# Combining the experts inside the second cross attention's program

## Chip, cores and metric

The kernel runs on one core of one Trainium2 chip. The metric is the device time of one execution in microseconds (us); lower is better. The engines are TensorE (PE in the profile; PEld is its weight load), VectorE (DVE), ScalarE (ACT), GpSimd (POOL) and SyncE (SP), which issues most of the DMAs. Each engine runs its own list of instructions in order; semaphores tie the lists together. SBUF is the memory on the chip, PSUM the banks into which TensorE writes.

## What is computed

A decoder of two layers over x, 4 x 1024 tokens of 256 numbers. Each half layer adds to x a function of its layer norm:

```python
x = x + _L0_xattn_ref(_layernorm(x), ctx, ctx, mask, ...)
x = x + _L0_ffn_ref(_layernorm(x), ...)      # self-attention, then one of 8 experts per token
x = x + _L1_xattn_ref(_layernorm(x), ctx, ctx, ...)
x = x + _L1_ffn_ref(_layernorm(x), ...)
```

What bears on the change is the end of the second and the start of the third:

```python
# end of _L0_ffn_ref: src is the attention's output, sel the chosen expert's row of each token
moe = sel * jnp.sum(wts, axis=-1, keepdims=True)
return _ln(src + moe, n2_g, n2_b)
# _L1_xattn_ref
query = _split_heads(q @ Wq + bq)            # q = _layernorm(x); 16 heads of 16
key_ = _split_heads(k @ Wk + bk)             # k = v = ctx, 64 rows per batch
value = _split_heads(v @ Wv + bv)
logits = jnp.einsum('bhqd,bhkd->bhqk', query, key_) / jnp.sqrt(DEPTH)
attn = jax.nn.softmax(logits, axis=-1)
out = jnp.einsum('bhqk,bhkd->bhqd', attn, value)
return concat @ Wo + bo
```

## The kernel before

x stays in SBUF as 32 tiles of 128 tokens; the stages go over it in eight chunks of four tiles (512 tokens). Each stage is a program of its own (a `Block`): all engines start it together and leave it together, and the semaphores are cleared in between.

`combine_experts` (names `co_`) ends the second half layer. SyncE loads the experts' rows chunk by chunk (`yg`), with the scale `n2g` after the second chunk and, behind all chunks, the seven tensors of the next cross attention's context (`Context.issue`: weights, transposed context, biases). VectorE forms z = rows x weight + src (`co_z`) and its moments, two chunks ahead of the rest; GpSimd makes the reciprocal deviation; VectorE turns mean and deviation into a shift; ScalarE normalizes z in place; GpSimd multiplies by `n2g`; VectorE adds z to x.

`cross_attention` (names `xa_`) follows. Its front: VectorE takes the moments of x, GpSimd makes `rstd`, VectorE normalizes x into `xn` (`normalize_x`), TensorE transposes it into the PSUM tile `front` (`transpose_xn`), ScalarE evacuates that to `xnT`, TensorE projects queries into the PSUM tile `rows` in two halves (`project_q`), ScalarE evacuates each half with its bias into `qT`. TensorE begins with the keys and values, which need only the context; ScalarE places the keys into a block form (`place_keys`) between the evacuations. TensorE's order is: transpose chunk 0; then for each chunk c transpose c+1, project c. A half of the projection waits for the evacuation of the same half one chunk earlier, since `rows` has one bank for each.

After the last projection come the four row maxima of chunk 0 (`scores` on TensorE, `maximum` on VectorE, turn by turn over the one tile `rows`), and then `attend(c)` for each chunk. It begins with `transpose_max`, writes the transposed scores to `cols`, and ScalarE makes the exponentials `pT`. GpSimd adds the output bias to x for all eight chunks (`add_output_bias`) after the last `rstd`.

The same function serves the first cross attention, which has a mask and takes x from the inputs.

Of the kernel before, what the change touches and what calls it, by code (L numbers as in the profile page):

```python
# [101 lines left out]
def cross_attention(nc, x_sb, k_, context, mask, name):  # L102
# [4 lines left out]
    with ExitStack() as ctx:  # L107
# [15 lines left out]
        qT = sb("qT", [P, HALVES, TOKENS])  # L123
# [6 lines left out]
        rden = sb("rden", [P, P])  # L130
        front = ps("front", [P, HALVES, CW])
# [14 lines left out]
        q_banks = [rows[:, half] for half in range(HALVES)]  # L146

        with nc.Block() as block:
            @block.sync
            def _(sp):  # L150
                if not context.issued:
                    context.issue(sp)
                if masked:
                    sp.dma_start(mask_i[:], mask.rearrange("(t p) k -> p t k", p=P)).then_inc(mask_loaded, 16)
# [3 lines left out]
            def _(dve):  # L158
# [95 lines left out]
                moments(0)  # L254
                moments(1)
                place_key_bias()
                for c in range(CHUNKS):
                    normalize_x(c)
                    if c == 0:
                        place_values()  # L260
                    if c + 2 < CHUNKS:
                        moments(c + 2)
                    if c == 1:
                        place_fill()
                for t in range(CT):
                    maximum(0, t)
# [8 lines left out]
            def _(pool):  # L275
# [40 lines left out]

                nc.gpsimd.memset(vblk[:], 0.0).then_inc(v_cleared, 1)
                for c in range(CHUNKS):
# [14 lines left out]
            def _(act):  # L333
# [6 lines left out]
                def evacuate_qT(c, half):  # L340
                    act.wait_ge(q_psum, 2 * c + half + 1)
                    nc.scalar.activation(qT[:, half, CW * c:CW * (c + 1)], q_banks[half], ACT.Identity,
# [33 lines left out]
                evacuate_xnT(0)  # L376
                act.wait_ge(context.loaded, context.count)
                act.wait_ge(kbias_made, 1)
                for c in range(CHUNKS):
# [24 lines left out]
            def _(pe):  # L404
# [27 lines left out]
                def scores(c, t):  # L432
# [9 lines left out]
                    for half in range(HALVES):  # L442
                        for r in range(2):
                            part = slice(SC * r, SC * (r + 1))
                            last = nc.tensor.matmul(rows[:, r, half * D:(half + 1) * D], qT[part, half, tokens],  # L445
# [15 lines left out]
                def weights_of(c, half):  # L461
# [9 lines left out]
                    for g in range(4):  # L471
                        part = slice(32 * g, 32 * (g + 1))
                        nc.tensor.matmul(cols[:, g], kblk[part, c // 2, half, 2 * g:2 * g + 2], qT[part, half, tokens],
# [79 lines left out]
                transpose_xn(0)  # L553
                for c in range(CHUNKS):
                    if c + 1 < CHUNKS:
                        transpose_xn(c + 1)
                    project_q(c)
# [9 lines left out]
                for t in range(CT):  # L567
# [2161 lines left out]
```

## Time and profile before

| | us |
|---|---|
| median of 3 runs (lowest to highest) | 1999.68 (1997.29 to 2002.81) |
| the profiled execution, its own time | 2008.15 |
| span of its trace | 2006.4 |
| combine_experts, from the engines' start on it to its last addition | 1397.8 to 1451.0 |
| change of program | 1451.0 to 1453.0 |
| front of the second cross attention | 1453.0 to 1507.0 |
| four maxima of its first chunk | 1507.0 to 1518.0 |
| its eight chunks of attention | 1518.0 to about 1668 |

Of these stretches the busy times are, for TensorE, 0, 0, 46.7, 5.5 and 139.6 us; for VectorE 45.6, 0, 39.6, 5.8 and 68.6 us.

A row of the views in order of time reads: start, duration, engine, line, operation, output<-inputs, shape, count of instructions merged into the row, and in brackets how long the engine had been idle before it and what ended that. Times are counted from the start of the span. Matmuls in fp32 appear as two instructions each, and their ends are modelled, so that neighbouring rows overlap a little. A row of the views by stretch gives the length, the busy time and count of each engine (PE, PEld, DVE, ACT, POOL), the granted TensorE clock as a share of full speed, the DMA share, and GB/s.

### The profile page before, as it was taken

What the parts mean: (1) busy time and instruction counts of PE and PEld (TensorE: products, weight loads), DVE (VectorE), ACT (ScalarE), POOL (GpSimd) and SP (SyncE); (2) the same over time, 40 slices, a digit from 0 to 9 for tenths busy, and PEclk for the clock granted to TensorE, in tenths of its full rate; (3) what the DMA queues carried; (4) which work ended last, traced back from release to release, by engine and by line L of the source; (5) the groups of instructions that cost most, each with busy time, mean ns of one, the idle gap of its engine ahead of it and who ended that gap; (6) DMA issues with size and microseconds to landing.
All of it is one profiled execution on the core that took longest, in us unless ns stands there. A gap on an engine that the chain in (4) does not pass through costs nothing. (4 is left out here: it accounts for less than half of the span.)

```text
span 2006.4 us, 30050 instructions
## 1 busy us (share of the span) xinstructions
PE 1703.1 (85%) x10580; PEld 805.3 (40%) x10580; DVE 1256.7 (63%) x2123; ACT 962.7 (48%) x1803; POOL 598.9 (30%) x645
## 2 busy tenths in 40 slices
PE   5899799899999999999997966996088996239996
PEld 3466454222222222222222653774054663125554
DVE  5344358788888888888860774664874545661221
ACT  2432245488888888888885422443342332102110
POOL 4300063242221121121121373665660002021533
PEclk8899999899999999999998977998588997658998
DMA  5000059532222322222102422222300004310542
GB/s 141 1 2 1 19 167 304 198 75 39 39 39 38 64 50 38 39 39 39 39 2 98 153 81 79 65 66 73 96 1 1 1 1 140 126 33 15 140 108 32
DMA packets 112677, 134.51 MB, mean 67 GB/s; under 512 B 18480, under 2 KB 88496, under 8 KB 112272
## 3 DMA queue, kind: packets, MB, share of 16 engines
q1 hardware_dynamic: 101824, 114.20, 20.8%
q0 software_dynamic: 9552, 17.83, 3.7%
q8 instruction: 87, 1.43, 0.3%
q10 hardware_dynamic: 1152, 0.54, 0.1%
q14 instruction: 62, 0.51, 0.1%
HBM read 78.47 MB, written 53.93 MB: 66 GB/s over the span
## 5 line engine op out<-in xcount | busy, mean ns | idle before, releaser
L892 DVE TENSOR_REDUCE sa_mhalf<-sa_a 128x2 f32<-128x1024 f32 x512 | 604.3, 1221 | 84.4 <-PE sa_a L1104 82.7
L1037 ACT ACTIVATE sa_e<-sa_b 128x512 f32<-128x512 f32 x683 | 383.4, 601 | 76.9 <-PE sa_b L1137 76.9
L1147 PE MATMUL sa_b2o<-sa_e,sa_v 128*17 128x512 f32 x2048 | 269.7, 598 | 0.0
L1037 ACT ACTIVATE sa_e<-sa_b2o 128x512 f32<-128x512 f32 x341 | 205.0, 601 | 40.6 <-PE sa_b2o L1137 40.6
L1137 PE MATMUL sa_b<-sa_q,sa_k 112*128 112x512 bf16 x468 | 163.4, 388 | 2.7 <-ACT sa_e L1037 2.7
L840 POOL TENSOR_TENSOR sa_rden<-sa_o_rows,sa_minus_one 128x16 f32<-128x16 f32 x32 | 93.0, 2908 | 178.1 <-ACT sa_o_rows L1020 178.1
L213 DVE TENSOR_REDUCE xa_mx<-xa_rows 128x16 f32<-128x1024 f32 x64 | 78.3, 1224 | 100.2 <-PE xa_rows L445 100.2
L1104 PE MATMUL sa_a<-sa_k,sa_q 48*128 48x512 bf16 x704 | 113.3, 389 | 13.2 <-DVE sa_mhalf L892 13.2
L829 POOL CAST sa_negm<-sa_neg 16x128 bf16<-16x128 f32 x32 | 9.4, 293 | 348.7 <-issue 338.9
L360 ACT ACTIVATE xa_pT<-xa_cols 128x1024 f32<-128x1024 f32 x64 | 62.1, 1022 | 84.5 <-PE xa_cols L477 84.5
L1137 PEld LDWEIGHTS sa_b<-sa_q,sa_k 112*128 112x128 bf16 x468 | 40.6, 97 | 151.2 <-ACT sa_e L1037 134.4
L1137 PE MATMUL sa_b2o<-sa_q,sa_k 112*128 112x512 bf16 x236 | 91.3, 387 | 0.6 <-ACT sa_e L1037 0.5
L2611 DVE TENSOR_TENSOR sw_hT<-sw_p,sw_act 128x512 f32<-128x512 f32 x32 | 22.1, 692 | 101.1 <-PE sw_p L2556 101.1
L2524 POOL DMA_INDIRECT out_x<-sw_yo,tc_idx x32 | 49.9, 1560 | 104.7 <-DVE sw_yo L2618 97.7
L1697 PE MATMUL ex_hps<-at_w,ex_xT 128*128 x156 | 77.3, 619 | 1.9 <-ACT ex_xT L1737 1.9
L445 PE MATMUL xa_rows<-xa_kblk,xa_qT 64*128 64x256 f32 x512 | 73.1, 407 | 6.1 <-DVE xa_mx L213 5.3
L1104 PEld LDWEIGHTS sa_a<-sa_k,sa_q 48*128 48x128 bf16 x704 | 30.5, 93 | 114.7 <-issue 56.7
L2600 ACT ACTIVATE sw_act<-sw_p 128x512 f32<-128x512 f32 x32 | 19.1, 597 | 118.0 <-PE sw_p L2550 115.2
L1720 PE MATMUL ex_yps<-at_attn,ex_hT 128*128 x312 | 74.0, 380 | 0.5 <-ACT ex_hT L1747 0.4
L544 PE MATMUL xa_cols<-c_ctxT,c_wts 128*128 128x256 f32 x16 | 7.5, 652 | 77.9 <-PEq L43 64.2
L1137 PE MATMUL sa_b<-sa_parts 112*128 112x512 bf16 x215 | 73.5, 384 | 0.0
L1747 ACT ACTIVATE ex_hT<-ex_tps,at_bt,at_g 128x128 f32<-128x128 f32 x156 | 58.8, 457 | 15.8 <-PE ex_tps L1708 15.8
(345 smaller groups left out, 3066.3 us busy)
## 6 DMA issues: line engine op xcount, KB each, us to landing
k_parts<-sa_parts SPq DMA_DIRECT2D x96, 128.0 KB, 2.2
tc_w<-in_L_ffn_W SPq DMA_DIRECT2D x24, 512.0 KB
sa_q<-q_parts SPq DMA_DIRECT2D x44, 192.0 KB, 5.4
sa_k<-k_parts SPq DMA_DIRECT2D x44, 192.0 KB, 5.8
q_parts<-sa_parts SPq DMA_DIRECT2D x16, 384.0 KB
ex_xg<-expert_in SPq DMA_DIRECT2D x39, 132.0 KB
v_groups<-sp_vt SPq DMA_DIRECT2D x8, 544.0 KB, 4.6
sa_v<-v_groups SPq DMA_DIRECT2D x16, 272.0 KB, 7.6
```

The source lines that it names most:

```text
L213: nc.vector.tensor_reduce(mx[:, t], rows[:].rearrange("p r (n k) -> p (r n) k", k=SC), axis=X, op=ALU.max).then_inc(max_done, 1)
L360: nc.scalar.activation(pT[:, 4 * half + 2 * part:4 * half + 2 * part + 2], cols[:, 2 * part:2 * part + 2], ACT.Exp, scale=SCALE).then_inc( ...
L445: last = nc.tensor.matmul(rows[:, r, half * D:(half + 1) * D], qT[part, half, tokens], kblk[part, c // 2, half, CT * r:CT * (r + 1)], star ...
L840: nc.gpsimd.tensor_tensor(rden[:], view[:, :, :, DK], minus_one[:], ALU.pow).then_inc(rden_made, 1)
L892: nc.vector.tensor_reduce(mhalf[a % 2][:, half, head:head + PAIRED + 1:PAIRED, t], aps[a_slot(use)][:], axis=X, op=ALU.max).then_inc(a_use ...
L1037: nc.scalar.activation(ex[(KT * n + kt) % (LAG + 1)][:, head], bps[use % 3], ACT.Exp, scale=SCALE).then_inc(b_used, 1)
L1104: last = nc.tensor.matmul(aps[a_slot(use)][:, h // PAIRED], qs[s][rows, h, q0:q0 + P], ks[s][rows, h, half * CW:(half + 1) * CW], start=Tr ...
L1137: nc.tensor.matmul(bps[use % 3], ks[s][:, head, kt * P:(kt + 1) * P], qs[s][:, head, qc * CW:(qc + 1) * CW], start=True, stop=True).then_i ...
L1147: last = nc.tensor.matmul(ops[32 * head:32 * head + VW], vs[s][:, kt, head], ex[(KT * n + kt) % (LAG + 1)][:, head], start=(kt == 0), stop ...
L1697: last = nc.tensor.matmul(hps[j % 2][:], xT[j % 2][:, half], ew["w1"][:, half, ds(e, 1), :], start=(half == 0), stop=(half == HALVES - 1))
L1720: last = nc.tensor.matmul(yps[j % 2][:, 0:D], hT[j % 2][:, f], ew["w2"][:, f, ds(e, 1), :], start=(f == 0), stop=(f == FK - 1))
L1747: last = nc.scalar.activation(hT[j % 2][:, f], tps[j % 2][:, f * P:(f + 1) * P], ACT.Gelu, bias=ew["bt"][:, f, ds(e, 1)], scale=ew["g"][:, ...
```

## The change

`combine_experts` is gone as a program. `cross_attention` gets an argument `combine`, which the second one is called with, and does the combination in its own program:

- z lies in what will be `pT`, the experts' rows in what will be `qT`, which is now ordered by chunk. The projection writes to the first two banks of `cols` in place of `rows`.
- SyncE issues the context's loads behind the third chunk of rows instead of behind the eighth.
- VectorE goes through steps: the shift of chunk s, the sum of chunk s+2, the addition to x and the moments of x for chunk s-1, a second shift (`xshift`) for chunk s-2. The key bias is made in step 2, the values placed in step 4, and from step 6 on each step ends with one maximum of chunk 0.
- ScalarE normalizes x too (`normalize_rows`, with `xshift`); before, VectorE did.
- ScalarE's step s is: normalize z of chunk s; in steps 2 and 3 place eight keys, in step 2 after waiting for the key bias; evacuate `xnT` of chunk s-3; normalize x of chunk s-2; evacuate the two query halves of chunk s-4.
- TensorE transposes chunk c, then projects chunk c; after chunks 1 to 4 the scores of one of chunk 0's four tiles follow.
- GpSimd makes the selector first, then the deviations of z and x and the multiplication, in steps; the two other constant shapes and the eight bias additions come after that.

The core of the diff:

```diff
-        qT = sb("qT", [P, HALVES, TOKENS])
+        qT = sb("qT", [P, CHUNKS, HALVES, CW])
...
-        q_banks = [rows[:, half] for half in range(HALVES)]
+        q_banks = [(cols if combine else rows)[:, half] for half in range(HALVES)]
...
+                if combine:
+                    for c in range(CHUNKS):
+                        sp.dma_start(yg[c], moe_out[CW * c:CW * (c + 1)].rearrange("(t p) d -> p t d", p=P)).then_inc(y_loaded[c], 16)
+                        if c == 1:
+                            sp.dma_start(n2g[:], n2_g.partition_broadcast(P)).then_inc(g_loaded, 16)
+                        if c == 2:
+                            context.issue(sp)
...
+                if combine:
+                    weighted_sum(0)
+                    weighted_sum(1)
+                    for step in range(CHUNKS + 2):
+                        if step < CHUNKS:
+                            make_shift(step)
+                        if step + 2 < CHUNKS:
+                            weighted_sum(step + 2)
+                        if 1 <= step <= CHUNKS:
+                            add_experts(step - 1)
+                            moments(step - 1)
+                        if step >= 2:
+                            make_x_shift(step - 2)
+                        if step == 2:
+                            place_key_bias()
+                        if step == 4:
+                            place_values()
+                        if step >= 6:
+                            maximum(0, step - 6)
...
+                    invert(0)
+                    pool.wait_ge(g_loaded, 16)
+                    for step in range(CHUNKS + 1):
+                        if step + 1 < CHUNKS:
+                            invert(step + 1)
+                        if step < CHUNKS:
+                            scale(step)
+                        if step >= 1:
+                            make_rstd(step - 1)
...
+                def normalize_rows(c):
+                    par = c % 2
+                    act.wait_ge(xshift_ready, c + 1)
+                    act.wait_ge(rstd_ready, c + 1)
+                    act.wait_ge(x_done, c + 1)
+                    if c >= 2:
+                        act.wait_ge(xnT_psum, c - 1)
+                    for t in range(CT):
+                        nc.scalar.activation(xn[:, par, t], x_sb[:, CT * c + t], ACT.Identity, bias=xshift[:, par, t:t + 1],
+                                             scale=rstd[:, par, t:t + 1]).then_inc(xn_ready, 1)
+
+                if combine:
+                    for step in range(CHUNKS + 4):
+                        if step < CHUNKS:
+                            normalize_z(step)
+                        if step == 2:
+                            act.wait_ge(kbias_made, 1)
+                        if 2 <= step < 4:
+                            act.wait_ge(k_psum, step - 1)
+                            for h in range(HH):
+                                place_keys(step - 2, h)
+                        if 3 <= step < CHUNKS + 3:
+                            evacuate_xnT(step - 3)
+                        if 2 <= step < CHUNKS + 2:
+                            normalize_rows(step - 2)
+                        if step >= 4:
+                            for half in range(HALVES):
+                                evacuate_qT(step - 4, half)
...
+                if combine:
+                    for c in range(CHUNKS):
+                        transpose_xn(c)
+                        if c == 0:
+                            pe.wait_ge(kblk_made, H)
+                        project_q(c)
+                        if 1 <= c <= CT:
+                            pe.wait_ge(qT_ready, HALVES)
+                            scores(0, c - 1)
+                else:
+                    transpose_xn(0)
+                    for c in range(CHUNKS):
+                        if c + 1 < CHUNKS:
+                            transpose_xn(c + 1)
+                        project_q(c)
```

On TensorE, from the key projection of the second cross attention, the order before is this (`xnT0` and `xnT1` are the two buffers of transposed x; the first entry of a row is the line, the last the count):

```order
L544 MATMUL xa1_cols<-c1_ctxT,c1_wts 128x256 x4
L550 MATMUL xa1_cols<-c1_wts,c1_ctxT 128x256 x8
L411 MATMUL xa1_front<-x_ident,xa1_xn 128x128 x16
L421 MATMUL xa1_rows<-xa1_xnT0,c1_wts 128x512 x4
L411 MATMUL xa1_front<-x_ident,xa1_xn 128x128 x8
L421 MATMUL xa1_rows<-xa1_xnT1,c1_wts 128x512 x4
```

Sixteen transposes, of chunks 0 and 1, stand ahead of the first projection. And now, at the same place:

```order
L693 MATMUL xa1_cols<-c1_ctxT,c1_wts 128x256 x4
L699 MATMUL xa1_cols<-c1_wts,c1_ctxT 128x256 x8
L560 MATMUL xa1_front<-x_ident,xa1_xn 128x128 x8
L570 MATMUL xa1_cols<-xa1_xnT0,c1_wts 128x512 x4
L560 MATMUL xa1_front<-x_ident,xa1_xn 128x128 x8
L570 MATMUL xa1_cols<-xa1_xnT1,c1_wts 128x512 x4
L594 MATMUL xa1_rows<-xa1_kblk,xa1_qT 128x256 x4
```

The transposes of chunk 1 have moved behind the projection of chunk 0, and scores follow the second projection.

On ScalarE, from the normalization of z, the order before is this:

```order
L1905 ACTIVATE co_z<-co_z,co_shift,co_rstd 128x256 x32
L1864 UNCONDITIONAL_BRANCH
L332 UNCONDITIONAL_BRANCH
L338 ACTIVATE xa_xnT<-xa_front 128x1024 x2
L342 ACTIVATE xa_qT<-xa_rows,c_bqk 128x512 x2
L347 ACTIVATE xa_kblk<-xa_cols,xa_kbias,x_headmask 128x4x64 x4
L338 ACTIVATE xa_xnT<-xa_front 128x1024
L342 ACTIVATE xa_qT<-xa_rows,c_bqk 128x512 x2
```

and now (z is `xa_pT`):

```order
L492 ACTIVATE xa_pT<-xa_pT,xa_shift,xa_zrstd 128x256 x12
L457 ACTIVATE xa_kblk<-xa_cols,xa_kbias,x_headmask 128x4x64 x8
L503 ACTIVATE xa_xn<-x_x,xa_xshift,xa_rstd 128x256 x4
L492 ACTIVATE xa_pT<-xa_pT,xa_shift,xa_zrstd 128x256 x4
L457 ACTIVATE xa_kblk<-xa_cols,xa_kbias,x_headmask 128x4x64 x8
L448 ACTIVATE xa_xnT<-xa_front 128x1024
L503 ACTIVATE xa_xn<-x_x,xa_xshift,xa_rstd 128x256 x4
L492 ACTIVATE xa_pT<-xa_pT,xa_shift,xa_zrstd 128x256 x4
L448 ACTIVATE xa_xnT<-xa_front 128x1024
L503 ACTIVATE xa_xn<-x_x,xa_xshift,xa_rstd 128x256 x4
L452 ACTIVATE xa_qT<-xa_cols,c_bqk 128x512 x2
```

All sixteen key placements now come ahead of the second evacuation of transposed x, and a normalization of x stands between each evacuation of transposed x and the evacuation of query halves.

On SyncE the context's loads stood behind the eighth chunk of rows:

```order
L1868 DMA co_yg<-moe_out 128x4x256 x2
L1871 DMA co_n2g<-in_L_ffn_n_g 128x256
L1868 DMA co_yg<-moe_out 128x4x256 x6
L98 DMA c_wts<-in_L_xattn_wts 128x8x256
L98 DMA c_ctxT<-in_ctxT 128x4x64 x4
```

and now they stand behind the third (the rows go into `xa_qT`):

```order
L164 DMA xa_qT<-moe_out 128x4x256
L98 DMA c_wts<-in_L_xattn_wts 128x8x256
L98 DMA c_ctxT<-in_ctxT 128x4x64 x4
L98 DMA c_bqk<-in_L_xattn_bqk 128x4
L98 DMA c_bv<-in_L_xattn_bv 128x256
L98 DMA c_bo<-in_L_xattn_bo 128x256
L164 DMA xa_qT<-moe_out 128x4x256 x5
```

The last five chunks have moved behind seven loads.

## Rows read from the trace of the kernel before

**Rows 1.** VectorE in order of time: start, us, engine, line, operation.

```profile
1401.76 1.67 DVE L1915 SCALAR_TENSOR_TENSOR co_z<-co_yg,sm_wsum,sm_src 128x256 f32<-128x256 f32 x4 [12.32 <-DMA co_yg<-moe_out]
...
1404.95 1.64 DVE L1915 SCALAR_TENSOR_TENSOR co_z<-co_yg,sm_wsum,sm_src 128x256 f32<-128x256 f32 x4
...
1415.99 2.39 DVE L1941 TENSOR_TENSOR x_x<-x_x,co_z 128x1024 f32<-128x1024 f32 x1
...
1441.85 1.23 DVE L1941 TENSOR_TENSOR x_x<-x_x,co_z 128x1024 f32<-128x1024 f32 x1
...
1453.04 1.41 DVE L188 BATCH_NORM_STATS2 xa_stats<-x_x 128x6 f32<-128x256 f32 x4 [2.06 <-PEq L43]
1454.36 0.37 DVE L194 BATCH_NORM_AGGREGATE xa_mv<-xa_stats 128x2 f32<-128x6 f32 x4
...
1481.60 14.89 DVE L203 TENSOR_SCALAR xa_xn<-x_x,xa_mv,xa_rstd 128x256 f32<-128x256 f32 x8 [0.78 <-PE xa_front L411]
```

**Rows 2.** ScalarE in order of time.

```profile
1408.26 2.07 ACT L1905 ACTIVATE co_z<-co_z,co_shift,co_rstd 128x256 f32<-128x256 f32 x4 [21.57 <-DVE co_shift L1933]
...
1467.77 1.02 ACT L338 ACTIVATE xa_xnT<-xa_front 128x1024 f32<-128x1024 f32 x1 [4.40 <-PE xa_front L411]
1470.29 0.69 ACT L342 ACTIVATE xa_qT<-xa_rows,c_bqk 128x512 f32<-128x512 f32 x1 [1.50 <-PE xa_rows L421]
...
1472.60 1.93 ACT L347 ACTIVATE xa_kblk<-xa_cols,xa_kbias,x_headmask 128x256 f32<-128x256 f32 x4
```

**Rows 3.** GpSimd in order of time.

```profile
1414.96 2.34 POOL L1888 TENSOR_TENSOR co_z<-co_z,co_n2g 128x1024 f32<-128x1024 f32 x1 [0.81 <-ACT co_z L1905]
...
1482.16 18.84 POOL L288 TENSOR_TENSOR x_x<-x_x,c_bo 128x1024 f32<-128x1024 f32 x8
```

**Rows 4.** TensorE in order of time, matmuls alone.

```profile
1453.04 3.75 PE L544 MATMUL xa_cols<-c_ctxT,c_wts 128*128 128x256 f32 x8 [64.22 <-PEq L43]
...
1465.76 1.89 PE L411 MATMUL xa_front<-x_ident,xa_xn 128*128 128x128 f32 x8 [3.45 <-DVE xa_xn L203]
1467.44 4.53 PE L421 MATMUL xa_rows<-xa_xnT,c_wts 128*128 128x512 f32 x8
1471.81 1.04 PE L411 MATMUL xa_front<-x_ident,xa_xn 128*128 128x128 f32 x8
1472.68 3.60 PE L421 MATMUL xa_rows<-xa_xnT,c_wts 128*128 128x512 f32 x8
...
1496.55 1.94 PE L411 MATMUL xa_front<-x_ident,xa_xn 128*128 128x128 f32 x8 [3.04 <-DVE xa_xn L203]
...
1506.97 1.14 PE L445 MATMUL xa_rows<-xa_kblk,xa_qT 64*128 64x256 f32 x8 [0.78 <-ACT xa_qT L342]
...
1514.35 2.08 PE L445 MATMUL xa_rows<-xa_kblk,xa_qT 64*128 64x256 f32 x8 [1.33 <-DVE xa_mx L213]
1518.02 2.08 PE L457 MATMUL xa_cols<-x_ident,xa_mxr 128*128 128x128 f32 x8 [1.59 <-DVE xa_mxr L216]
...
1522.04 2.05 PE L473 MATMUL xa_cols<-xa_qT,xa_kblk 32*128 32x512 f32 x8
...
1527.11 1.14 PE L473 MATMUL xa_cols<-xa_qT,xa_kblk 32*128 32x512 f32 x8 [1.10 <-ACT xa_pT L360]
...
1536.23 1.16 PE L457 MATMUL xa_cols<-x_ident,xa_mxr 128*128 128x128 f32 x8
```

**Rows 5.** SyncE's queue: start, time on the queue, DMA.

```profile
1408.53 7.32 SPq L98 DMA_DIRECT2D c_ctxT<-in_ctxT  x4
```

**Rows 6.** Stretches: length, busy of five engines, clock share, DMA share, GB/s.

```profile
1397.00:1405.00 8.00, 0.00 (x0) 0.00 (x0) 3.24 (x13) 0.00 (x0) 0.00 (x0) 0.50 0.62 190
1411.00:1413.00 2.00, 0.00 (x0) 0.00 (x0) 1.96 (x7) 0.19 (x1) 1.92 (x3) 0.50 1.10 348
1467.00:1469.00 2.00, 2.00 (x6) 1.12 (x5) 2.00 (x10) 1.02 (x1) 1.55 (x5) 0.50 0.00 0
1469.00:1471.00 2.00, 2.00 (x6) 0.89 (x5) 2.00 (x10) 0.69 (x1) 1.64 (x3) 0.92 0.00 0
```

More of the change, by code:

```diff
@@ new lines, in _ @@
+                if combine:
[18 more added lines that the diff above has]
+                else:
+                    moments(0)
+                    moments(1)
+                    place_key_bias()
+                    for c in range(CHUNKS):
+                        normalize_x(c)
+                        if c == 0:
+                            place_values()
+                        if c + 2 < CHUNKS:
+                            moments(c + 2)
+                        if c == 1:
+                            place_fill()
+                    for t in range(CT):
+                        maximum(0, t)
@@ L374, in evacuate_mT, with normalize_z @@
                     nc.scalar.activation(mT[:], cols[:, 0], ACT.Copy).then_inc(mT_ready, 1)
[L376 to L379, printed above, removed]
+                def normalize_z(c):
+                    par = c % 2
+                    act.wait_ge(shift_ready, c + 1)
+                    act.wait_ge(zrstd_ready, c + 1)
+                    act.wait_ge(z_ready, CT * (c + 1))
+                    for t in range(CT):
+                        nc.scalar.activation(z[c % 4][:, t], z[c % 4][:, t], ACT.Identity, bias=shift[:, par, t:t + 1],
+                                             scale=zrstd[:, par, t:t + 1]).then_inc(zn_ready, 1)
@@ L380, in _ @@
+                for c in range(0 if combine else CHUNKS):
                     if c + 1 < CHUNKS:
@@ L444, in scores @@
                             part = slice(SC * r, SC * (r + 1))
-                            last = nc.tensor.matmul(rows[:, r, half * D:(half + 1) * D], qT[part, half, tokens],
+                            last = nc.tensor.matmul(rows[:, r, half * D:(half + 1) * D], qT[part, c, half, t * P:(t + 1) * P],
                                                     kblk[part, c // 2, half, CT * r:CT * (r + 1)],
@@ L566, in _ @@
                         transpose_fill(c)
-                for t in range(CT):
-                    scores(0, t)
+                if not combine:
+                    for t in range(CT):
+                        scores(0, t)
                 for c in range(CHUNKS):
```

201 lines of the change are left out of this document (82 added, 119 removed).

## The prediction, made before the change was run

> **What bounds the kernel now.** I read the views in this order: the busy time of the stages, then each engine in order of time between 1397 and 1545 us, then the SyncE queue and the DMA rate in the same stretch. Three stages lie there one after the other. The combination of experts runs from 1401.8 to 1451 us and is VectorE's, eight chunks in 49 us, while TensorE does nothing. Then comes a change of program of 2.0 us, up to the row of 1453.04 [rows 1]. The front of the second cross attention (normalize, transpose, project queries) runs from there; in it TensorE is the bound where all goes well, since transposes and projection of a chunk follow each other without a hole at 1.04 + 3.60 us, less their overlap, 4.3 us a chunk [rows 4]. From 1506.97 TensorE and VectorE take turns over the first four maxima. The attention proper begins with the transposes of the maxima at 1518.02 us, and from there TensorE is nearly always busy until the stage ends. So the whole change is worth what it does to that one moment, 1518.02, and to the clock TensorE has at it.
>
> **Prices.** A chunk's weighted sum with its moments takes VectorE 3.2 us (1401.76 to 1404.95); adding the experts' part 1.23 us alone and 2.39 us when GpSimd multiplies at the same time (2.34 us) [rows 1, 3]; the moments of x 1.7 us (statistics 1.41, aggregates 0.37) [rows 1]. ScalarE: four normalizations 2.07, an evacuation of transposed x 1.02, one of a query half 0.69, four key placements 1.93 us [rows 2]. The normalization of x moves to ScalarE; on that engine no row shows it, but four activations of the same 128x256 shape are the row of 2.07. On VectorE the last eight took 14.89 us, because GpSimd's bias additions ran beside them (18.84 us for eight) [rows 1, 3].
>
> **The part up to the first transposes.** VectorE's first 6.4 us stay. On the SyncE queue the context's seven loads now stand between the third and fourth chunk of expert rows (before, the context's four largest pieces alone kept it 7.32 us [rows 5]). Until chunk 3 is in, three chunks of 0.52 MB (512 x 256 fp32), 0.13 for the scale, 1.84 for the context (1.05 weights, 0.52 transposed context, 0.26 biases) and 0.52 must be moved: 4.06 MB. By 1405 about 1.5 MB had been moved (8 us at 190 GB/s), the rest at 348 GB/s takes 7.3 us [rows 6]: 1412.3, and with some 3 us until a landing is seen I take 1415.5. VectorE wants it at 1413.4. Bounds: 1412, no wait at all, to 1419, if the queue issues the context as slowly as before. GpSimd's multiplication of chunk 1 then holds the sums off to about 1418, so step 1 ends at 1423.7 (3.2 + 1.2 + 1.7). Step 2 is a shift 0.2, a chunk 3.2, the addition 3.0 with its wait for GpSimd, moments 1.7, two small ones 0.4: 1432.2. Only then is the key bias made, for which ScalarE waits (queued behind it are the normalization of x and the next z, for which GpSimd waits in turn). Eight key placements 3.9 and the normalization 2.07: first transposes at 1438.2. The second eight placements and the next z come before the first evacuation, so the first projection begins at 1445.1. The key and value projections, at the front's head before (3.75 us the keys alone [rows 4]), vanish into this time.
>
> **The loop that is new.** Before, TensorE transposes chunk c+1 ahead of projecting chunk c. Now it transposes c, projects c. On ScalarE a step is: next z, evacuate transposed x of c, normalize x of c+1, evacuate the queries of c-1. The projection of c needs both the first and the last of these. Nothing overlaps: projection P, scores S, transposes T, then 1.02 + 2.07 + 0.69 us of ScalarE with TensorE idle, plus some 0.1 for each of the hand-overs. The next z is hidden behind P and S. VectorE needs 8 us a step (3.2 + 1.2 to 2.4 + 1.7 + small ones + a maximum later on) and hides behind this loop, if that is over 8 us.
>
> How long P is hangs on the clock. TensorE stands idle 3.8 us in each turn. After idle times of 3.45 and 3.04 us it came back at half clock: transposes 1.89 and 1.94 us instead of 1.04 [rows 4], granted clock 0.50, that is 1.2 GHz, and 0.92 in the next two microseconds, mostly 2.4 GHz [rows 6]. The first of these slow phases ran from 1465.76 to about 1469.2. So I take P as four matmuls at the slow pitch and four at the fast, 3.44 + 1.72 = 5.16 us, and T and S fast, 1.04 and 1.13. A turn is then 11.1 us with scores, 10.0 without.
> The sum: 1445.1 + 5.1 (first P) = 1450.2; four turns with scores, 44.4: 1494.6; two without, 20.0: 1514.6; last turn without a normalization and with the last evacuation, 8.6: **1523.2 us** for the transposes of the maxima, against 1518.02. That is +5.2.
>
> **What is given back.** Before, TensorE came to 1518.02 from waiting for maxima and ran slow to about 1524: transposes 2.08, scores 2.08, weights 2.05 against 1.16, 1.13 and 1.14 at full clock [rows 4]. Now it comes from its last projection after 0.8 us and should be fast: -2.8 us. All four maxima are done by 1497, so their turns (11 us before) are gone, inside the sum above. The eight bias additions wait for the last normalization, 1508.7, and end near 1514, before the attention; nobody waits. Other edits (query tile ordered by chunk, query banks in another bank, tiles shared with the probabilities) change no count: 0. The first cross attention keeps its order.
>
> Net +2.4 us on the profiled execution's 2008.15 us (span 2006.4). That execution is 8.5 us above the median of the runs; I add the difference to the median: 1999.68 + 2.4 = **2002.1 us**, forecast 2002. A measurement of this kernel tells about 0.3%, 6 us, from no change.
>
> **Two rules weighed.** An addition with two SBUF inputs took 2.39 us beside GpSimd and 1.23 alone [rows 1]. The Trainium skill (Advanced Engine Details and Errata, Mode Summary under VectorE Performance Modes) says that GpSimd and two-port Vector instructions block each other; a fp32 addition is not in such a mode, so by the page's wording the additions would cost 1.2 us each here, 9 us less over the eight. The trace is against that; either way the sum stays, as VectorE hides behind the loop.
> TensorE returned from 3.45 us of idleness at 0.50 of its clock. The Trainium skill (TensorE: Matmul & The Clock Gate, Part 1) says the slow state is the default and activity releases it; by it, too, each turn would begin slow, and rival A would not come.
>
> **Rivals.**
> A. The idle 3.8 us does not cost the clock, whatever the two holes above did. For it: at the maxima TensorE, idle 1.33 us before every 1.13 us of scores, was still fast for some 7 us after 1506.97 and slow only at 1514.35 [rows 4]. Against: that end, and both longer holes. P is then 3.44 (3.60 less its tail), eight times 1.72 us less, 13.8: 1988.
> B, the slower side: the slow phase lasts longer than those 3.4 us. For it: after 1518.02 it lasted 5.9 us of nearly full work. Then 1.2 us more for each of eight turns, +10: 2012. At its worst the clock never rises in the loop: P 6.9, T 1.94, S 2.08, turns of 14.6, the end at 1547 and 2026 to 2029. It decides as soon as P and the rest of a turn lie wholly in the slow phase.
> C. The change does what one would hope, and VectorE sets the pace: some way out of the loop that I missed, steps of 8 us from 1401.8 on, maxima transposed near 1495, some 25 us less: 1975. Against it stand the order of ScalarE's four items and the waits of the projection; only if the normalization of x were not in front of the queries' evacuation would it come near.
> D. The context's loads are not late (1412) or much later (1419): -3 or +3.5 on any of these.
>
> **How the numbers follow.** Forecast with D around it, 1996 to 2008: 0.48. A, 1985 to 1991: 0.20. B, 2006 to 2018: 0.20, and its worst, near 2027: 0.06. C: 0.06. The range of 8 in 10 leaves out C and B's worst and the tail of B: 1986 to 2013. Faster by over 0.3% (under 1993.7): A and C, 0.27. Slower (over 2005.7): B, its worst, and a fifth of the forecast's spread, 0.35. Within: 0.38; the likeliest case alone reaches 1996 to 2008.
>
> **What would show it.** The transposes of queries' input should start one per 10 to 11 us, each followed by 3.7 us of idle TensorE that ends on a query evacuation by ScalarE; first transposes near 1438, those of the maxima near 1523 on the same axis; half clock at the head of each projection and 1.16 us transposes of maxima. Turns of 9.4 us would be A, 12 to 15 us B, 8 us C. I am wrong from the ground up if TensorE is not idle between transposes and projection of one chunk, or if the fourth chunk's rows hold VectorE up for more than some 6 us.

## The result, and the profile after

| | before | after |
|---|---|---|
| median of 20 runs each | 1998.66 us | 2003.03 us |
| lowest to highest | 1994.37 to 2003.10 | 2001.66 to 2008.08 |
| ratio, 95% interval | | 1.0023 (1.0016 to 1.0030) |
| profiled execution, its span | see the table ahead | 2005.57, 2003.8 us |

The change costs 4.6 us (3.2 to 6.0). 2002.0 us was forecast, and a time within 0.3% of before was the likeliest sign. The span of the profiled execution of after is 2.6 us *shorter* than that of before, against the medians. In the profiled execution of before TensorE stalls for some 11 us between 1778 and 1792 us, in the routing stage, which the change does not touch and where after has no such stall. It is not the change that removes it: a second trace of the changed kernel, taken later, runs 330.6 us from the first transposes of the next program to its end, as before does (330.7), against 320.1 in this one. So nothing is read from whole spans here; all readings are of the stretch around the second cross attention.

TensorE, second cross attention of the changed kernel, in order of time (start, us, line, operation, idle before it and what ended it). It answers to [rows 4].

```profile
1439.24 1.97 PE L560 MATMUL xa_front<-x_ident,xa_xn 128*128 128x128 f32 x8 [15.60 <-ACT xa_xn L503]
1445.83 5.99 PE L570 MATMUL xa_cols<-xa_xnT,c_wts 128*128 128x512 f32 x8 [4.62 <-ACT xa_xnT L448]
1451.66 1.04 PE L560 MATMUL xa_front<-x_ident,xa_xn 128*128 128x128 f32 x8
1456.43 5.37 PE L570 MATMUL xa_cols<-xa_xnT,c_wts 128*128 128x512 f32 x8 [3.74 <-ACT xa_qT L452]
1461.73 1.14 PE L594 MATMUL xa_rows<-xa_kblk,xa_qT 64*128 64x256 f32 x8
1462.79 1.09 PE L560 MATMUL xa_front<-x_ident,xa_xn 128*128 128x128 f32 x8
...
1478.79 6.58 PE L570 MATMUL xa_cols<-xa_xnT,c_wts 128*128 128x512 f32 x8 [3.73 <-ACT xa_qT L452]
...
1502.38 6.73 PE L570 MATMUL xa_cols<-xa_xnT,c_wts 128*128 128x512 f32 x8 [3.73 <-ACT xa_qT L452]
1508.95 1.04 PE L560 MATMUL xa_front<-x_ident,xa_xn 128*128 128x128 f32 x8
1513.72 3.67 PE L570 MATMUL xa_cols<-xa_xnT,c_wts 128*128 128x512 f32 x8 [3.74 <-ACT xa_qT L452]
1517.23 1.04 PE L560 MATMUL xa_front<-x_ident,xa_xn 128*128 128x128 f32 x8
1520.05 3.67 PE L570 MATMUL xa_cols<-xa_xnT,c_wts 128*128 128x512 f32 x8 [1.78 <-ACT xa_qT L452]
1524.50 1.16 PE L606 MATMUL xa_cols<-x_ident,xa_mxr 128*128 128x128 f32 x8 [0.78 <-ACT xa_qT L452]
```

Each chunk is now transposed and then projected, and between the two TensorE stands idle 3.7 us, ended by ScalarE's evacuation of query halves. Before, no such hole stood there: 1471.81 and 1472.68 follow each other [rows 4]. The transposes of the maxima, with which the attention proper begins, come at 1524.50.

ScalarE of the same kernel shows what fills the hole.

```profile
1463.93 1.02 ACT L448 ACTIVATE xa_xnT<-xa_front 128x1024 f32<-128x1024 f32 x1 [5.10 <-PE xa_front L560]
1464.85 2.06 ACT L503 ACTIVATE xa_xn<-x_x,xa_xshift,xa_rstd 128x256 f32<-128x256 f32 x4
1466.81 1.24 ACT L452 ACTIVATE xa_qT<-xa_cols,c_bqk 128x512 f32<-128x512 f32 x2
```

Evacuation of transposed x, normalization of the next x, evacuation of the queries: 1.02 and 2.06 us, and half of 1.24, whose first half frees the bank for the projection at 1467.62.

SyncE's queue and VectorE answer to [rows 5] and [rows 1]: first the loads, then VectorE's sums.

```profile
1399.51 0.94 SPq L164 DMA_DIRECT2D xa_qT<-moe_out  x2
1400.50 0.50 SPq L166 DMA_DIRECT2D xa_n2g<-in_L_ffn_n_g  x1
1401.04 1.76 SPq L164 DMA_DIRECT2D xa_qT<-moe_out  x1
1402.84 0.51 SPq L98 DMA_DIRECT2D c_wts<-in_L_xattn_wts  x1
1403.39 6.65 SPq L98 DMA_DIRECT2D c_ctxT<-in_ctxT  x4
...
1412.09 5.35 SPq L164 DMA_DIRECT2D xa_qT<-moe_out  x5
```

```profile
1404.99 1.67 DVE L276 SCALAR_TENSOR_TENSOR xa_pT<-xa_qT,sm_wsum,sm_src 128x256 f32<-128x256 f32 x4 [13.91 <-DMA xa_qT<-moe_out]
...
1418.65 3.48 DVE L276 SCALAR_TENSOR_TENSOR xa_pT<-xa_qT,sm_wsum,sm_src 128x256 f32<-128x256 f32 x4 [2.58 <-DMA xa_qT<-moe_out]
...
1429.83 1.19 DVE L300 TENSOR_TENSOR x_x<-x_x,xa_pT 128x1024 f32<-128x1024 f32 x1
```

The fourth chunk's rows leave the queue at 1412.09 and hold VectorE up for 2.58 us. From here on times are counted from SyncE's first load of rows, 1397.88 us before and 1399.51 after, so that what the earlier stages do by chance falls away.

| stretch | before | after | difference |
|---|---|---|---|
| first load to transposes of the first maxima | 120.14 | 124.99 | +4.85 |
| from there to the next such transposes (1536.23 and 1539.93) | 18.21 | 15.43 | -2.78 |
| from there to the last output projection | 126.31 | 126.29 | -0.02 |
| from there to the first transposes of the next program | 13.14 | 17.51 | +4.37 |
| sum | | | +6.42 |

The times say +4.6 (3.2 to 6.0), so 1.8 us of this sum are not in them, and no trace shows where they went. The second timing of the unaltered changed kernel (below, among the experiments) gave +6.4 us (4.4 to 8.4), which is the sum. The last stretch, +4.37, was not in the prediction. Last output projection and first transposes of the next program, after:

```profile
1666.22 6.75 PE L663 MATMUL xa_front<-c_wts,xa_oS 128*128 128x256 f32 x16 [1.31 <-DVE xa_oS L246]
1683.73 1.94 PE L2259 MATMUL ts_tps<-x_ident,ts_xn 128*128 128x128 f32 x8 [10.77 <-DVE ts_xn L2205]
```

and before:

```profile
1662.54 3.72 PE L514 MATMUL xa_front<-c_wts,xa_oS 128*128 128x256 f32 x16 [1.31 <-DVE xa_oS L228]
1675.68 1.94 PE L2208 MATMUL ts_tps<-x_ident,ts_xn 128*128 128x128 f32 x8 [9.42 <-DVE ts_xn L2154]
```

The projection runs at half the pace (+3.0 us), and the change of program that follows takes 1.35 us more. All of that lies between VectorE's last row of the one program and its first of the next: 3.53 us before, 4.87 after.

### The profile page after: what moved, and what is told of

Same layout as the page of the kernel before. It is cut to its first block and busy times, and to the rows that moved or that the text cites. A ratio compares the mean times of both kernels' runs of the same rounds, so it can differ in the third digit from the quotient of the medians.

```text
span 2003.8 us, 30074 instructions
## 1 busy us (share of the span) xinstructions
PE 1712.3 (85%) x10579; PEld 808.8 (40%) x10580; DVE 1230.8 (61%) x2099; ACT 976.6 (49%) x1835; POOL 600.8 (30%) x645
## 3 DMA queue, kind: packets, MB, share of 16 engines
q8 instruction: 87, 1.43, 0.3%
## 5 line engine op out<-in xcount | busy, mean ns | idle before, releaser
L570 PE MATMUL xa_cols<-xa_xnT,c_wts 128*128 128x512 f32 x64 | 42.7, 830 | 28.8 <-ACT xa_qT L452 24.2
```

## The experiments

**How they are given.** They ran in three sets, each on another chip, and each set beside the kernel before, whose median there was 2011.2 us (matmuls in the hole, queries first, transposes ahead, context last), 2009.7 us (both orders, the two with the maxima behind, transposes ahead with the context last) and 2012.0 us (the changed kernel again, context last again, the key bias). Each is given by its ratio to the kernel before in the same comparison, and that ratio times 1998.7 us, so that it stands beside 2003.0 of after. "The stretch" is from SyncE's first load of rows to the transposes of the first maxima: 124.99 us after, 120.14 before. It repeated to 0.05 us in the second trace of the changed kernel, so that differences between sets are read from it rather than from the times.

**The theory.** TensorE, ScalarE and the projection form one serial loop of 10 to 11 us a chunk; its length is TensorE's own work, the idle 3.7 us, and what the clock costs after it. Rivals: VectorE sets the pace (8 us steps) and the loop only looks serial; or the context's loads and late key bias hold all up.

### The clock's share: 2.6 us of matmuls in each hole

The matmuls write an unused bank, and read what was projected before.

```
     if c == 0:
         pe.wait_ge(kblk_made, H)
+    else:
+        pe.wait_ge(v_made, 2 * B)
+        for i in range(3):
+            nc.tensor.matmul(cols[:, 3], wts[:, 0, 0, 0:P], xnT[(c - 1) % 2][:, 0], start=True, stop=True)
     project_q(c)
```

> The changed kernel, with three matmuls of 128x512 added per turn ahead of each projection but the first, written to an unused bank: 2.6 us of work at full clock in TensorE's idle 3.7 us. They are extra work that nobody reads. Clock term of the prediction (each turn begins at half clock because TensorE has been idle): the idle time nearly gone, projections take 3.6 instead of 5.4 to 6.6 us, turns of 9.4 us, some 12 us less than the changed kernel, about 1991 us. Rival, that the slow matmuls are not a matter of idle time: 2003 us with projections of 5.4 us, or up to 2010 where fillers at half clock (5.2 us) stick out of the hole.

Measured: ratio 0.9971 (0.9951 to 0.9990), 1992.9 us, 10 us less than after though TensorE does more. The stretch is 114.3 us, 10.7 less. TensorE, one turn of it:

```profile
1470.88 1.09 PE L561 MATMUL xa_front<-x_ident,xa_xn 128*128 128x128 f32 x8
1471.81 2.74 PE L711 MATMUL xa_cols<-xa_xnT,c_wts 128*128 128x512 f32 x6
1475.70 3.67 PE L571 MATMUL xa_cols<-xa_xnT,c_wts 128*128 128x512 f32 x8 [1.16 <-ACT xa_qT L453]
1479.31 1.14 PE L595 MATMUL xa_rows<-xa_kblk,xa_qT 64*128 64x256 f32 x8
1480.37 1.09 PE L561 MATMUL xa_front<-x_ident,xa_xn 128*128 128x128 f32 x8
```

The turn is 9.5 us: TensorE's own work at full clock and the hole of ScalarE's three items, of which 2.74 us are now filled and 1.16 are not. Every projection after the first takes 3.67 us or less. The eight projections of after sum to 42.7 us, these to 31.8: the difference of 10.9 accounts for the 10.7 us of the stretch. This is what the clock costs in the loop. The idle time itself stays a part of the turn.

### ScalarE's order: the queries out first

```
+    if step >= 4:
+        for half in range(HALVES):
+            evacuate_qT(step - 4, half)
     if 2 <= step < CHUNKS + 2:
         normalize_rows(step - 2)
-    if step >= 4:
-        for half in range(HALVES):
-            evacuate_qT(step - 4, half)
```

> The changed kernel, with one order altered on ScalarE: in each step the two query halves of chunk c-1 are evacuated before x of chunk c+1 is normalized, not after. Serial-loop theory: the projection of c no longer waits behind 2.07 us of normalization, TensorE's idle time between transposes and projection falls from 3.7 to about 1.7 us in each of seven turns, and being short it should no longer bring half clock: turns of 8.2 us with scores, 6.1 without, maxima transposed some 20 us earlier than in the changed kernel, about 1983 us (before 1998.7, changed 2003.0). Rival, that VectorE's added work (additions, moments of x, second shift, maxima) paces the turns: the order on ScalarE changes nothing of note, 2001 to 2004 us, turns stay near 11 us and VectorE has no idle time in them.

Measured: 0.9925 (0.9899 to 0.9951), 1983.7 us; the stretch 103.9. Two turns:

```profile
1461.28 3.67 PE L570 MATMUL xa_cols<-xa_xnT,c_wts 128*128 128x512 f32 x8 [1.78 <-ACT xa_qT L452]
1465.53 1.13 PE L594 MATMUL xa_rows<-xa_kblk,xa_qT 64*128 64x256 f32 x8 [0.58 <-DVE xa_mx L231]
1466.60 1.09 PE L560 MATMUL xa_front<-x_ident,xa_xn 128*128 128x128 f32 x8
1469.47 5.37 PE L570 MATMUL xa_cols<-xa_xnT,c_wts 128*128 128x512 f32 x8 [1.78 <-ACT xa_qT L452]
```

The hole shrinks by the 2 us of the normalization, from 3.74 to 1.78, and only one projection after the first is still slow (5.37). Of the 21 us some 12 are the shorter holes and 10 the projections (32.8 us for all eight instead of 42.7). In two turns the scores now wait for VectorE's maximum (0.58 and 0.57 us): VectorE has come close. Not VectorE but this order set the 11 us; the rival falls.

### TensorE's order: transposes one chunk ahead

```
+    transpose_xn(0)
     for c in range(CHUNKS):
-        transpose_xn(c)
+        if c + 1 < CHUNKS:
+            transpose_xn(c + 1)
         if c == 0:
             pe.wait_ge(kblk_made, H)
         project_q(c)
```

> The changed kernel, with TensorE's old order: the transposes of chunk c+1 stand ahead of the projection of chunk c. Serial-loop theory: evacuation of transposed x, next z and normalization (5 us of ScalarE) run beside a projection; TensorE waits only for the query evacuation (about 1.3 us); turns become 5 to 7 us, set by ScalarE and VectorE in turn; maxima transposed some 28 us earlier than in the changed kernel, about 1975 us. It also ends the half clock. Rival, VectorE's pace of 8 us a step: turns of 8 us, 2003 - 7 x 3 = about 1982 us. Rival, that the order is nothing and the common program costs by contention: 2000 us or more.

Measured: 0.9872 (0.9837 to 0.9906), 1973 us; the stretch 92.6.

```profile
1473.47 3.60 PE L570 MATMUL xa_cols<-xa_xnT,c_wts 128*128 128x512 f32 x8
1477.01 1.13 PE L594 MATMUL xa_rows<-xa_kblk,xa_qT 64*128 64x256 f32 x8
1478.07 1.09 PE L560 MATMUL xa_front<-x_ident,xa_xn 128*128 128x128 f32 x8
1479.00 3.60 PE L570 MATMUL xa_cols<-xa_xnT,c_wts 128*128 128x512 f32 x8
```

No hole is left in these turns; a turn is 5.53 us. So the order that the change gave up on TensorE (it is how the kernel before does it) is worth 30 us here by the ratios (23 to 37 with their intervals), 32.4 by the stretch. From the fourth chunk on nothing holds TensorE up.

### Both orders

> The changed kernel with both orders altered: transposes of c+1 ahead of the projection of c, and queries evacuated before x is normalized. The two are not additive by the serial-loop theory: with the transposes ahead, ScalarE in front of a query evacuation would wait for the projection while the normalization of the next x, for which the next transposes wait, stands queued behind it. The loop closes again through the normalization: projection 3.5, queries 1.2, normalization 2.0, transposes 1.0, evacuation after: turns of 7.2 us, maxima transposed some 8 us later than with the transposes ahead alone, about 1982 us (that kernel: 1973 on the same scale). Rival, that each removes its own wait and they add up: under 1970 us.

Measured: 0.9926 (0.9904 to 0.9949), 1983.9 us; the stretch 104.3. Together they are 11 us worse than transposes ahead alone by the ratios, whose intervals just touch, and 11.8 by the stretches. ScalarE:

```profile
1467.15 0.69 ACT L452 ACTIVATE xa_qT<-xa_cols,c_bqk 128x512 f32<-128x512 f32 x1 [1.03 <-PE xa_cols L570]
1467.74 2.06 ACT L503 ACTIVATE xa_xn<-x_x,xa_xshift,xa_rstd 128x256 f32<-128x256 f32 x4
```

With transposes ahead, ScalarE reaches the queries before TensorE has finished them. It waits, and the normalization that TensorE's next transposes need stands behind that wait: turns of 7.27 us, with 1.68 us of idle TensorE. An order that is right for one neighbour is wrong for the other.

### The maxima moved back behind the projections

Scores and maxima of the first group leave the loops and run one after the other behind them, as before the change.

```
     project_q(c)
-    if 1 <= c <= CT:
-        pe.wait_ge(qT_ready, HALVES)
-        scores(0, c - 1)
...
+for t in range(CT):
+    scores(0, t)
```

> The changed kernel, with the four first maxima taken after all projections, as in the kernel before (the rest of the change stays). Serial-loop theory: four turns lose their scores, 1.07 us each, 4.3 us; after the last projection four rounds of scores and maximum come, 2.46 us each and one transfer, 10 us, and TensorE goes into the attention from waiting, so at half clock as in the kernel before, 3 us more. About +6 to +9 us on the changed kernel, 2009 to 2012 us: this part of the change is worth that much. Rival, that the maxima lengthen each VectorE step and the turns with it: turns shorter by 2.5 us, about 2003 us.

Measured: 1.0064 (1.0047 to 1.0081), 2011.5 us; the stretch 129.9, and from there to the next transposes of maxima 17.0 instead of 15.4.

```profile
1516.89 1.13 PE L592 MATMUL xa_rows<-xa_kblk,xa_qT 64*128 64x256 f32 x8 [0.78 <-ACT xa_qT L450]
1519.42 1.13 PE L592 MATMUL xa_rows<-xa_kblk,xa_qT 64*128 64x256 f32 x8 [1.40 <-DVE xa_mx L231]
1521.88 2.00 PE L592 MATMUL xa_rows<-xa_kblk,xa_qT 64*128 64x256 f32 x8 [1.33 <-DVE xa_mx L231]
...
1528.87 2.08 PE L604 MATMUL xa_cols<-x_ident,xa_mxr 128*128 128x128 f32 x8 [1.59 <-DVE xa_mxr L234]
```

The taking of turns costs 12.0 us (1516.89 to 1528.87; 11.05 before, 1506.97 to 1518.02) and leaves the clock at half, as in [rows 4]. The loop itself ends earlier, 117.9 us after the first load, since turns of 10 us replace those of 11 and no later projection takes more than 5.4 us.

### Transposes ahead, maxima behind

> Transposes ahead and the four maxima after all projections: the common program alone, without its second idea. Without the serial loop the maxima among the projections should be worth their full 10 us: 1973 + 10 and up to 3 more for half clock behind them, 1983 to 1986 us. Rival, that they delay the projections about as much as they save at the end, since each scores waits for VectorE: under 1977 us.

Measured: 0.9935 (0.9915 to 0.9955), 1985.7 us; the stretch 103.2. With this run the two choices make a square (us against the kernel before, all with the combination in the program):

| | maxima in the loop | maxima behind it |
|---|---|---|
| transposes just ahead of their projection | +4.6 (the change) | +12.8 |
| transposes one chunk ahead | -25.6 | -13.0 |

The maxima in the loop are worth 8 us in one order and 13 in the other. The four times come from three chips, and their intervals are 1.4 to 7 us wide to either side; the traces, read from the first load to the first transposes of the next program, give 5.1 and 13.4 us. The combination by itself, with TensorE's old order, is worth 13 us. The change gained both, and lost 30 us by the transposes.

### The context's loads after all rows

```
-    if c == 2:
-        context.issue(sp)
```

> The changed kernel, with the context's seven loads behind all eight chunks of expert rows, as in the kernel before. Term D of the prediction: VectorE no longer waits for the fourth chunk (2.58 us in the changed kernel's trace) nor meets GpSimd's multiplication with it (sums of 3.48 instead of 1.67 us); everything behind comes 3 to 4 us earlier: about 1999.5 us. Rival, that the late rows are hidden since ScalarE waits for the key bias anyway: 2003 us, or later if the keys' projection, now some 8 us later, is what the key placements wait for.

Measured: 1.0019 (1.0002 to 1.0037), 2002.5 us; the stretch 121.5. The trace shows the 3.5 us, the time does not tell 3.5 us from nothing: its interval covers that of after. So both ran again beside each other, five rounds each.

> The changed kernel itself, unaltered, timed on the same chip as the two that follow, so that the context's late loads can be told from it. Expected 1.0023 times the kernel before, as when it was first timed, with the interval overlapping 1.0016 to 1.0030; from SyncE's first load of rows to the transposes of the maxima 125 us again, turns of 11.1 us. If its trace differs from the first by microseconds in the turns, the lengths of the slow-clock phases are no property of the program and no turn should be read singly.

> The change with the context's seven loads issued after all rows, timed beside the changed kernel itself. Theory 1 (the loads hold up the fourth chunk and the whole chain): from the first load to the transposes of the maxima 121.5 us against 125, and 3.5 us less in the time, a ratio to the kernel before lower by 0.0017. Theory 2 (what is gained at the head is lost again where the context's weights land later or at the end of the stage): the same 3.5 us in the stretch, and no more than 1 us in the time. Theory 3: the 3.5 us lie within what the chain moves by chance, and neither shows.

Measured: the changed kernel 1.0032 (1.0022 to 1.0042; at first 1.0023, 1.0016 to 1.0030), its stretch 124.9; with the context last 1.0005 (0.9997 to 1.0014), its stretch 121.5. The intervals no longer touch, and the difference is 5.4 us by the ratios and 4.0 by the medians (2017.05 and 2013.07): the loads' place costs some 4 us. The traces give 3.4. The first comparison, with an interval of 3.5 us to either side, was too coarse to show it.

The second run of the unaltered kernel also gave its projections again: 6.05, 5.37, 5.37, 6.59, 5.37, 6.73, 3.67, 3.67 us, against 5.99, 5.37, 5.34, 6.58, 5.37, 6.73, 3.67, 3.67 the first time. The long ones at 6.6 and 6.7 and the fast seventh are no accident of a run; they belong to this sequence of work.

### Putting it together

Transposes ahead and the context's loads last:

> Transposes of c+1 ahead of the projection of c, and the context's loads behind all expert rows. Term D: the fourth chunk is no longer late, 3 us off the start of the loop, and nothing else waits for the context: about 1970 us, maxima transposed 89 to 90 us after SyncE's first load (92.6 with the transposes ahead alone). Rival, that the key placements now wait for the key projection, which starts some 8 us later: no gain, 1973 us.

Measured: 0.9840 (0.9823 to 0.9856), **1966.7 us**, 32 us under before; the stretch 89.1. This is the fastest kernel of the study. A third step, the key bias made at the head of step 2, was tried on top:

```
     if step < CHUNKS:
         make_shift(step)
+    if step == 2:
+        place_key_bias()
     if step + 2 < CHUNKS:
         weighted_sum(step + 2)
```

> Three steps together: transposes one chunk ahead of the projections, the context's loads last, and the key bias made on VectorE at the head of step 2, ahead of the weighted sum of chunk 4, so that ScalarE's sixteen key placements need not wait for the end of that step. From the first load to the transposes of the maxima 89.1 us with the first two steps. Theory 1 (ScalarE's wait for the key bias is on the chain that starts the loop): some 3 us sooner, 86 us, ratio 0.9825. Theory 2 (the loop is by now at VectorE's pace, and VectorE only does the same work in another order, 0.4 us sooner or later): 89 us, ratio 0.984 as before. Rival on the other side: the context has not landed when the bias is wanted, VectorE waits for the bias loads, and the sums behind it start later, 92 us, 0.9855.

Measured: 0.9847 (0.9833 to 0.9860), 1968.1 us; the stretch 91.6. The time tells no difference. The stretch is that of the rival (92), but not by its reason: VectorE did not wait for the bias loads (the key bias is made at 1422.84, without idle time before it). The first transposes did come sooner, 33.8 us after the first load instead of 36.0, but then VectorE's addition fell onto GpSimd's scaling (2.93 us, at 1452.05), where in the kernel without this step it did not (1.19):

```profile
1452.05 2.93 DVE L298 TENSOR_TENSOR x_x<-x_x,xa_pT 128x1024 f32<-128x1024 f32 x1
```

```profile
1458.91 1.97 PE L558 MATMUL xa_front<-x_ident,xa_xn 128*128 128x128 f32 x8 [4.81 <-ACT xa_xn L501]
```

and TensorE waits 4.8 us for that chunk, 2.0 in the kernel without the step. Once the loop is short, VectorE's steps are on the path and their overlaps count. The two traces divide the 2.5 us: the second shift behind this addition ends 1.70 us later after the first load, and so do these transposes begin (59.55 against 57.85 us); the projection behind them takes 5.21 us instead of 4.39, another 0.82. The addition is not alone in the 1.70: a shift before it, at 1444.10, took 1.97 us instead of 0.13 beside the previous multiplication, and the next shift, at 1448.67, took 0.16 instead of 1.43.

## Why the prediction was right, and where its numbers were off

**Bound and place.** The prediction rested the whole change on the transposes of the first maxima, and on the clock there. The stretches bear this out up to the last output projection: +4.85 against +5.2 forecast, then -2.78 against -2.8, then nothing.

**The first transposes.** Forecast 40.3 us after the first load, measured 39.7. Two errors lie inside it and nearly cancel. The first rows landed 5.5 us after their issue (1399.51 to 1404.99), not 3.9 as before (1397.88 to 1401.76 [rows 1]), which the sum did not have. Against that, the additions of the eight chunks took 1.2 us each. Seven of them had no multiplication beside them; the one of step 2, at 1429.83, started together with GpSimd's multiplication, and it was GpSimd that waited. The first row is the multiplication beside the sums of 1418.65, the second the one beside this addition:

```profile
1418.32 2.34 POOL L408 TENSOR_TENSOR xa_pT<-xa_pT,xa_n2g 128x1024 f32<-128x1024 f32 x1 [0.91 <-ACT xa_pT L492]
...
1429.83 3.40 POOL L408 TENSOR_TENSOR xa_pT<-xa_pT,xa_n2g 128x1024 f32<-128x1024 f32 x1
```

3.40 us instead of 2.34 [rows 3], longer by about the addition. The sum had 3.0 us for this addition, so that here the rule that was weighed did not leave the sum as it was: ahead of the loop VectorE is not hidden. The two engines do hold each other up, and either can pay. Where the multiplication had begun first, by 0.33 us at 1418.32 and by 0.50 in the kernel with the key bias, VectorE paid (3.48 us for sums of 1.67; 2.93 for an addition of 1.2). Where both began together GpSimd paid. No run has a case in which VectorE clearly began first. The Trainium skill has the hold-up of such instructions in another place than the one the prediction weighed: GPSIMD Engine Reference, Specifications, lists contention with VectorE instructions in a two-port mode "or with two SBUF inputs". The trace agrees: the sums and the additions have two inputs in SBUF.

**Term D, the context's loads.** Forecast a wait of VectorE of 2 us, from 1413.4 to 1415.5; it waited 2.58. The bound below zero was right in kind too: moved away, the stretch is 3.5 us shorter, against 3 forecast.

**The loop.** Forecast hole 3.8 us, measured 3.73 or 3.74 in six turns. Forecast turns 11.1 four times, 10.0 twice, 8.6: 73.0 us. Measured 11.13, 11.17, 12.40, 11.20, 11.39, 8.28, 7.27: 72.8. The projection was sized at 5.16 us throughout. It took 5.37 where the clock rose halfway, 6.58 and 6.73 in two turns where it rose late, and 3.67 in the last two, where the clock never fell although TensorE had been idle 3.74 us before the first of them (1.78 before the second). So rival B (the slow phase lasts longer) came true in two turns, rival A (the hole costs no clock) in one hole of 3.74 us and in the shorter last one, and they about cancelled. That each turn would begin slow, as the second rule weighed had it, failed there. The mechanism was right; the even size of P was not, and that the total came out right to 0.2 us owes something to luck. By the run with matmuls in the hole the clock cost 10.9 us, of the 13.8 that separated forecast and rival A.

The granted clock (PEclk, third from the right, ahead of DMA share and GB/s) shows when it is lost, first around the projection that took 5.34 us, then around the one of 6.58:

```profile
1462.00:1464.00 2.00, 1.89 (x16) 1.27 (x14) 1.97 (x5) 0.07 (x1) 1.84 (x3) 1.00 0.00 0
1466.00:1468.00 2.00, 0.38 (x1) 0.41 (x2) 1.02 (x6) 2.00 (x5) 0.00 (x0) 0.90 0.00 0
1468.00:1470.00 2.00, 2.00 (x3) 0.77 (x3) 0.92 (x3) 2.00 (x5) 0.00 (x0) 0.50 0.00 0
...
1476.00:1478.00 2.00, 0.00 (x0) 0.00 (x0) 0.00 (x0) 2.00 (x6) 0.00 (x0) 0.96 0.00 0
1478.00:1480.00 2.00, 1.21 (x2) 0.73 (x3) 1.83 (x7) 2.00 (x5) 0.00 (x0) 0.50 0.00 0
```

In the first it is at 1.00 through the transposes and the hole, and 0.50 (1.2 GHz) as the projection begins at 1467.62. In the second it falls at about 1477.7, inside the hole, 1.1 us before the projection at 1478.79. In slices of half a microsecond it was at half for 3.4 us in each of the three turns that cost 1.7 us, and for 7.0 and 6.8 us in the two that cost 2.9 and 3.1. It fell from 1.1 us before the projection's start to 0.9 after it. It always rose while TensorE was at work.

**Rival C.** "Some way out of the loop that I missed" did not exist in the changed kernel, but one line away from it: 1975 was its price, 1973 was measured with the transposes ahead. That the two agree is luck: the price was VectorE's steps of 8 us from the first rows on, and the turns there are 5.5 us from the fourth chunk on. What the prediction named as the way there, the normalization out of the queries' way, gave 1983.7; the stronger lever was on TensorE, and the prediction did not see it, though it had shown both orders side by side.

**What was missing.** The end of the stage: 3.0 us for an output projection at half clock and 1.35 us for the change of program, 4.4 us together. The forecast of +2.4 is short of the measured +4.6 (3.2 to 6.0) by about half of that. The projection is at half clock in both traces of the changed kernel (6.75 and 6.74), likewise in both runs with only the context moved (6.75 and 6.74); it takes 5.10 to 5.39 us in three variants and 3.72 in the other five. It repeats with the kernel, from chip to chip, and differs between variants whose rows from the second transposes of maxima to this projection keep their times to 0.03 us, so it goes with what ran before; by what rule is open. The longer change of program, 10.76 to 10.79 us of idleness instead of 9.42, is in every variant of the changed program. Why is open. The cross attention's program now has 19 more semaphores to be cleared at its end; that this is the reason was not tested.

**Waits forecast and seen.** VectorE hid behind the loop: from 1461 to 1484 us it waited 2.9 to 3.7 us a step for GpSimd's z, as at 1461.41, and 2.8 and more for ScalarE to release the tile of normalized x, as at 1466.94:

```profile
1461.41 1.25 DVE L300 TENSOR_TENSOR x_x<-x_x,xa_pT 128x1024 f32<-128x1024 f32 x1 [2.92 <-POOL xa_pT L408]
...
1466.94 0.38 DVE L212 BATCH_NORM_AGGREGATE xa_mv<-xa_stats 128x2 f32<-128x6 f32 x4 [2.84 <-ACT xa_xn L503]
```

The bias additions ended at 1515.8, ahead of the attention, and cost nothing.

## What to carry to other kernels

When two stages are merged, count for each engine which item must wait for which of its neighbours, and close the circle: a chain that returns to its start within one chunk (transpose, evacuate, normalize, evacuate, project) sets the pace however little any engine is busy, and working one chunk ahead on one engine opens it. Change one order at a time, since the best order of ScalarE here turned with TensorE's. Work out what each small hole costs in clock as well as in time, by filling it once with idle matmuls.

## What the runs showed that was not expected

- A hole of the same 3.74 us cost TensorE 1.7 us of clock in some turns, 2.9 to 3.1 in two, and nothing in one; a hole of 1.78 us cost 1.7 in one turn of the kernel with the queries first and nothing in the others. The same kernel repeats its pattern to 0.06 us. No length of hole decides by itself.
- Three superfluous matmuls a turn, 2.74 us of TensorE, made the kernel 10 us faster.
- The first rows of a stage landed 3.9 us after their issue in the kernel before and 4.5 to 5.8 in the twelve traces of the changed program, with the same loads in the queue's first three places. With the context last, which leaves the same order of loads as before, it was 4.9 to 5.0. Why is open.
- An overlap of VectorE and GpSimd is paid by the one or by the other: 1.19 and 3.40 us in one place, 2.93 and 2.35 in another, 3.48 and 2.34 in a third.
